# Attention's score loop in phases of three tiles, with part of the fills moved to VectorE

## What is computed

```python
x = L0_attn_x                                    # (8, 1024, 256) float32
x = x + 0.5 * ffn(_layernorm(x), ...)            # 8 experts, top 2, and a shared one
x = x + attn(_layernorm(x), ...)
x = x + 0.5 * ffn(_layernorm(x), ...)

def attn(x, ...):                                # H, DH = 16, 64
    h = layernorm(x) * ln_scale + ln_bias
    c_q, c_kv = h @ w_down_q.T, h @ w_down_kv.T  # 256 -> 128 each
    q, k = rope(heads(c_q @ w_up_q.T)), rope(heads(c_kv @ w_up_k.T))
    v = heads(c_kv @ w_up_v.T)
    attn = softmax(q @ k.T / 8, axis=-1)         # 1024 x 1024 for each head
    return (attn @ v).reshape(b, s, H * DH) @ w_out.T + x
```

## Time and profile before

| | us |
|---|---|
| time, median of 3 runs | 4272.12 (4264.85 to 4278.15) |
| the profiled execution's own time | 4275.68 |
| its span in the trace | 4273.9 |
| attention, first to last fill | 584.5 to 3708.0 |
| one period of attention | 6.11 |

### The profile page before, as it was taken

One profiled execution on the slowest core, in us unless ns is written; L12 is line 12 of the kernel. 1 busy time (PEld: TensorE's weight loads), 2 busy tenths in 40 slices (PEclk: granted clock), 3 DMA queues, 4 the chain that ended last, 5 costly groups with the idle time before them and its releaser, 6 DMA issues. The chain is left out here.

```text
span 4273.9 us, 65982 instructions
## 1 busy us (share of the span) xinstructions
PE 3974.6 (93%) x24896; PEld 2240.6 (52%) x24896; DVE 2681.9 (63%) x3451; ACT 3002.4 (70%) x3792; POOL 3043.7 (71%) x1642
## 2 busy tenths in 40 slices
PE   7999979999999999999998999999999999779999
PEld 6888834444444444444444444444444444368888
DVE  5556567666656666766666666667766666255663
ACT  4444458777877787787778787878787778634454
POOL 3444458778888887887788888878888888624444
PEclk9999989999999999999999999999999999889999
DMA  3333221112111211121112112111211222123331
GB/s 105 107 119 110 72 89 58 53 53 80 53 51 55 76 53 54 60 70 51 59 60 65 63 51 70 58 53 57 79 50 51 66 68 63 31 94 119 119 110 60
DMA packets 194222, 301.07 MB, mean 70 GB/s; under 512 B 51470, under 2 KB 102256, under 8 KB 193264
## 3 DMA queue, kind: packets, MB, share of 16 engines
q1 hardware_dynamic: 193904, 296.86, 21.5%
HBM read 201.86 MB, written 26.74 MB: 53 GB/s over the span
## 5 line engine op out<-in xcount | busy, mean ns | idle before, releaser
L1032 DVE TENSOR_REDUCE atNM<-atPS 128x2 f32<-128x1024 f32 x1024 | 1208.0, 1219 | 788.3 <-PE atPS L848 784.6
L1115 POOL TENSOR_TENSOR atACC<-atACC,atPT 128x1024 f32<-128x1024 f32 x512 | 1290.7, 2521 | 64.3 <-ACT atPT L970 10.3
L970 ACT ACTIVATE atPT<-atPS 128x1024 f32<-128x1024 f32 x1024 | 992.6, 1022 | 201.5 <-PE atPS L869 196.4
L961 ACT ACTIVATE atPS<-atSH 128x1024 f32<-128x1024 f32 x1024 | 1008.7, 1022 | 29.3 <-DMA atSH<-atMD 21.8
L880 PE MATMUL atPO<-atPT,atV 128*64 128x512 f32 x4096 | 980.2, 600 | 0.0
L1115 POOL TENSOR_TENSOR atACC<-atPT 128x1024 f32<-128x1024 f32 x256 | 617.7, 2413 | 145.2 <-PE atOT L891 124.5
L848 PE MATMUL atPS<-atKH,atQH 64*128 64x512 f32 x2048 | 462.3, 449 | 163.6 <-ACT atPT L970 137.3
L1094 POOL TENSOR_TENSOR atVT<-atVT,atSIN 128x512 f32<-128x512 f32 x254 | 347.0, 1366 | 301.1 <-DMA atVT<-atR 300.8
L880 PEld LDWEIGHTS atPO<-atPT,atV 128*64 128x64 f32 x4096 | 283.1, 138 | 482.2 <-issue 475.6
L869 PE MATMUL atPS<-atQH,atKL 64*128 64x512 f32 x2048 | 468.7, 454 | 25.9 <-ACT atPS L961 25.9
L848 PEld LDWEIGHTS atPS<-atKH,atQH 64*128 64x128 f32 x2048 | 194.4, 186 | 413.5 <-ACT atPT L970 349.3
(11 more groups left out here) (275 smaller groups left out, 6552.3 us busy)
## 6 DMA issues: line engine op xcount, KB each, us to landing
atSH<-atMD SPq DMA_DIRECT2D x128, 512.0 KB, 4.4
atVT<-atR SPq DMA_DIRECT2D x508, 128.0 KB, 2.0
f1GB<-f1GD SPq DMA_DIRECT2D x128, 256.0 KB, 6.9
atRSUM<-atRD SPq DMA_DIRECT2D x128, 256.0 KB, 3.9
f2GB<-f2GD SPq DMA_DIRECT2D x128, 256.0 KB, 6.9
X<-x SPq DMA_DIRECT2D x4, 1024.0 KB, 6.0
XS<-x SPq DMA_DIRECT2D x16, 256.0 KB, 3.5
atRQ<-atRSUM SPq DMA_DIRECT2D x256, 4.0 KB, 1.8
```

The lines of the kernel that those rows point to most:

```text
L961: act.eng.activation(PS[ring.of[("score", n, t, j)]][:, :, :], SH[t][:, :, :], ACT.Copy).then_inc(filled[j % 2].sem)
L970: act.eng.activation(PT[k % NPT][:, :, :], PS[ring.of[step]][:, :, :], ACT.Exp, scale=SCALE).then_inc(grown.sem)
L1032: dve.eng.tensor_reduce(NM[:, q // 4, :, q % 4, t], PS[ring.of[step]][:, :, :], AX.X, ALU.max, negate=True).then_inc(most_out.sem)
L1115: pool.eng.tensor_tensor(total[:, :, :], begun[:, :, :], PT[k % NPT][:, :, :], ALU.add).then_inc(gathered.sem)
```

## The change

The list is built from phases of three tiles. With x as the running number of a tile (16 for each head), one turn of the new loop stands for three tiles: score x, maximum, score x + 1; then the others of tick x, the fill of x + 2 and the attend of x - 1; then maximum, score x + 2, maximum; then the others of tick x + 1, the fills of x + 3 and x + 4, the attends of x and x + 1, and the others of tick x + 2. Each old period is two ticks: `begin` and `early` go to the even one, `late` and `end` to the odd one. The maxima run 14 tiles ahead of the scores. `high` of the keys moves from tick 0 to the tick in front, `high` of the queries from the end of the period to tick 0. Key tiles 3 and 7 are filled by VectorE, with a semaphore of their own. `norm` works on one tile at a time at eight periods, not on two at four. `NAT` is 4. The core of the diff:

```diff
-    NAT = 3
+    NAT = 4
...
-                        for i in range(4):
-                            at(end, m, -33 + i, ("norm", b, i))
+                        for k in range(T):
+                            at(end, m, -33 + k, ("norm", b, k))
...
-                at(early, m, 0, ("high", m, 1))
-                at(end, m, 0, ("high", m, 0), ("klow", m))
+                at(end, m, -1, ("high", m, 1))
+                at(early, m, 0, ("high", m, 0))
+                at(end, m, 0, ("klow", m))
...
+            def tile(name, x):
+                n, r = divmod(x, 2 * T)
+                return [(name, n, r // T, r % T)] if 0 <= n < NN else []
+
+            def most_of(x):
+                n, r = divmod(x + 14, 2 * T)
+                return [("most", n, r // 2, r % 2)] if 0 <= n < NN else []
...
-            for g in range(-PER * 2 - 2, PER * NN + 3 * PER):
...
-                order += begin.get(g, []) + scores + mosts + early.get(g, []) + fills + attends
-                order += [("gather",) + s[1:] for s in attends if s[3] % 4] + late.get(g, []) + end.get(g, [])
+            for x in range(-42, 2 * PER * (NN + 4), 3):
+                order += tile("score", x) + most_of(x) + tile("score", x + 1)
+                order += others_of(x) + tile("fill", x + 2) + tile("attend", x - 1)
+                order += [step for step in tile("gather", x - 1) if step[3] % 4]
+                order += most_of(x + 1) + tile("score", x + 2) + most_of(x + 2)
+                order += others_of(x + 1) + tile("fill", x + 3) + tile("fill", x + 4) + tile("attend", x) + tile("attend", x + 1)
+                order += [step for i in range(2) for step in tile("gather", x + i) if step[3] % 4] + others_of(x + 2)
...
+            def filler(j):
+                return 2 if j % 4 == 3 else j % 2
...
+                    elif name == "fill" and filler(step[3]) == 2:
+                        _, n, t, j = step
+                        before = ring.before[("score", n, t, j)]
+                        dve.wait_ge(*shift[t](n))
+                        dve.wait_ge(*(grown if before[0] == "score" else most_out)(*before[1:]))
+                        dve.eng.tensor_copy(PS[ring.of[("score", n, t, j)]][:, :, :], SH[t][:, :, :]).then_inc(filled[2].sem)
```

More of the change, by code:

```diff
@@ L630, in attention @@
             PER = 8
-            begin, early, late, end = {}, {}, {}, {}
+            begin, early, late, end = ((0, 0), {}), ((0, 1), {}), ((1, 0), {}), ((1, 1), {})
             def at(table, m, period, *steps):
-                table.setdefault(PER * (m - 1) + period, []).extend(steps)
+                (tick, _), steps_of = table
+                steps_of.setdefault(2 * (PER * (m - 1) + period) + tick, []).extend(steps)
             TURNS = [(-21, late), (-20, late), (-17, early), (-17, late), (-9, early), (-9, late), (-8, early), (-8, late)]
@@ L680, in attention @@
                 at(end, NN - 4, 3 + i, ("stats", NB, i))
-                at(end, NN - 4, 10 + i, ("norm", NB, i))
+            for k in range(T):
+                at(end, NN - 4, 10 + k, ("norm", NB, k))
             at(end, NN - 4, 7, ("spread", NB))
-            order = []
-            for g in range(-PER * 2 - 2, PER * NN + 3 * PER):
-                n, r = divmod(g, PER)
-                t, pair = r // 4, (2 * (r % 4), 2 * (r % 4) + 1)
-                scores = [("score", n, t, j) for j in pair] if 0 <= n < NN else []
-                n1, r1 = divmod(g - 1, PER)
-                attends = [("attend", n1, r1 // 4, 2 * (r1 % 4) + i) for i in range(2)] if 0 <= n1 < NN else []
-                m, q = divmod(g - 1, PER)
-                mosts = [("most", m + 1, q, i) for i in range(2)] if 0 <= m + 1 < NN else []
-                n2, r2 = divmod(g + 1, PER)
-                fills = [("fill", n2, r2 // 4, 2 * (r2 % 4) + i) for i in range(2)] if 0 <= n2 < NN else []
-                order += begin.get(g, []) + scores + mosts + early.get(g, []) + fills + attends
-                order += [("gather",) + s[1:] for s in attends if s[3] % 4] + late.get(g, []) + end.get(g, [])
+            def tile(name, x):
+                n, r = divmod(x, 2 * T)
+                return [(name, n, r // T, r % T)] if 0 <= n < NN else []
@@ new lines, in most_of, with others_of @@
+            def most_of(x):
+                n, r = divmod(x + 14, 2 * T)
+                return [("most", n, r // 2, r % 2)] if 0 <= n < NN else []
+            def others_of(x):
+                return [step for (tick, _), table in (begin, early, late, end) if tick == x % 2 for step in table.pop(x, [])]
+            order = []
+            for x in range(-42, 2 * PER * (NN + 4), 3):
[5 more added lines that the diff above has]
+                order += [step for i in range(2) for step in tile("gather", x + i) if step[3] % 4] + others_of(x + 2)
@@ L698, in events @@
+            assert not any(table for _, table in (begin, early, late, end))
             def events(*names):
                 return [step[1:] for step in order if step[0] in names]
+            def filler(j):
+                return 2 if j % 4 == 3 else j % 2
             SEQ = {(0, 0): 0, (1, 0): 1, (1, 1): 2, (0, 1): 3}
@@ L734, in attention @@
             shift = [sig(f"shift{t}", 16).expect(heads) for t in range(2)]
-            filled = [sig(f"filled{i}").expect([s for s in events("fill") if s[2] % 2 == i]) for i in range(2)]
+            filled = [sig(f"filled{i}").expect([s for s in events("fill") if filler(s[2]) == i]) for i in range(3)]
             score, grown = (sig(x).expect(events("score")) for x in ("score", "grown"))
@@ L916, in scalar @@
                         act.wait_ge(*turned(b - 1, 1, 1))
-                        for k in (2 * i, 2 * i + 1):
-                            one, two = (slice(x * T + k, x * T + k + 1) for x in range(2))
-                            ins = act.eng.activation(Y[:, k, :], X[:, k, :], ACT.Identity, scale=A[:, two], bias=B[:, two])
-                            if b < NB:
-                                ins = act.eng.activation(X[:, k, :], X[:, k, :], ACT.Identity, scale=A[:, one], bias=B[:, one])
-                        if i == 3:
+                        one, two = (slice(x * T + k, x * T + k + 1) for x in range(2))
+                        ins = act.eng.activation(Y[:, k, :], X[:, k, :], ACT.Identity, scale=A[:, two], bias=B[:, two])
+                        if b < NB:
+                            ins = act.eng.activation(X[:, k, :], X[:, k, :], ACT.Identity, scale=A[:, one], bias=B[:, one])
+                        if k == T - 1:
                             ins.then_inc(normed.sem)
@@ L955, in scalar @@
                         act.eng.activation(ML[t][:, :], OT[0:8, 0:128], ACT.Copy).then_inc(row_out.sem)
-                    elif name == "fill":
+                    elif name == "fill" and filler(step[3]) < 2:
                         _, n, t, j = step
@@ L1147, in sync @@
                         sp.wait_ge(*written(n, t))
-                        for i in range(2):
-                            sp.wait_ge(*filled[i].past(n - 1, t, T - 2 + i))
+                        for j in range(T - 3, T):
+                            sp.wait_ge(*filled[filler(j)].past(n - 1, t, j))
                         sp.eng.dma_start(SH[t][:, :, :].rearrange("p h q -> p (h q)"),
```

6 lines of the change are left out of this document (3 added, 3 removed).

## The result

| | us |
|---|---|
| changed kernel, median of 4 runs | 4487.9 (4485.7 to 4498.3) |
| kernel before, on the same chip | 4269.1 (4264.9 to 4278.2) |
| ratio, 95% interval | 1.0514 (1.0489 to 1.0539) |
| profiled execution, changed | 4498.3, span 4496.5 |
| predicted | 4430 (4240 to 4560) |

The kernel is 5.1% slower. The sign and the place were forecast; the loss is 219 us, not 160.

What follows compares the result with a forecast made beforehand. TensorE plus one wait per period was taken as the bound. Per triple, -0.78 - 0.12 + 0.90 + 0.42 + 0.05 = +0.47 us, x 341 = +160 us, gave 4430 us, range 4240 to 4560.

Steps and rivals of the forecast that it cites:

- The sign and the place: Slower, chance 0.75; in attention, the fill of the middle score of the second phase (B) comes late.
- the clock: Rival: TensorE idles more and part of attention runs at 1.2 GHz; a tenth would cost some 290 us; chance 0.03.
- -0.78: TensorE's work for three tiles in attention falls from 6.56 to 5.78 us, the mid-phase wait for exponentials gone.
- gap A: After phase A (score, maximum, score), with one attend: B's middle score waits for its fill, 0.90 us per triple.
- gap B: After phase B (maximum, score, maximum), with two attends: late fills and accumulator copies cost 0.42 us per triple.
- -0.12 for earlier roundings: At head starts, TensorE's waits for the rounded queries go away, 0.12 us per triple.
- the 9.64 of the forecast: Predicted time of one triple (three tiles) in attention, 9.64 us, against 9.17 before.
- tick 8: Triples starting at this tick: a rotation stands before VectorE's fill and makes it late, 1.5 us.
- The neighbourhood of attends 7 and 0: At ticks 7 and 15 the second attend waits for ScalarE's copy of the accumulator, 1.3 and 1.9 us.
- the forecast's 0.47: Net loss per triple in attention, +0.47 us, times 341 triples +160 us.
- VectorE's fill: VectorE's 128x1024 copy from SBUF to PSUM, not in the trace, taken at 1.21 us like the reduction.
- my rival on the faster side: Phases cover the fill of B's middle score, waits under 0.85 us a triple; 153 us faster, 4120 us; chance 0.17.

Runs made afterwards that it cites:

- VectorE's fills first: Changed kernel with only VectorE's fills moved in front of the other steps of their tick, ScalarE's still behind them: 4415.8 us, ratio 1.0336.
- three moves: Changed kernel with the broadcast right behind the write, the accumulator's copy before ScalarE's fills, VectorE's fills before the other steps: 4349.6 us, ratio 1.0188.

## Why the prediction was right, and where it was not

**Right: the mechanism and the place.** The wait for exponentials fell to 4.1 us, and in its place scores wait for fills and attends for the copy. The size, 4488 against 4430, owes part to luck: the waits were taken too large, which nearly cancels a gain taken too large, and the clock was left out.

**What goes away: too large.** The wait itself was 137.3 - 4.1 = 133 us, 0.39 us a triple. The forecast's -0.78 also took TensorE's own work in the new order at 5.78 us. The first score and maximum of a triple hold to it: 1.03 us forecast, 1.07 on average. But in the plain place above, the work of gap A takes 2.13 us (2743.39 to 2745.52), not 1.96, since the switch to an attend and back takes 0.17 us that I left out. In gap B at ticks 1 and 5, where nothing waits, the forecast's terms give 2.79 + 0.93 + 0.20 = 3.92 us (values, a row) and 2.79 + 0.91 + 0.91 = 4.61 (a projection, half an output projection); measured are 4.07 and 4.68. So the gain was taken too large by about 0.3 us a triple.

**The roundings: not shown.** The -0.12 for earlier roundings did take away a wait of before, 14.5 us in all:

```profile
PE atPS L848 <- ACT atQH L950: 14.5, 25, 0.6
```

But in the old order the same edit, together with the fourth buffer that was priced at nothing, cost 32 us. No run shows the 41 us that 0.12 a triple would be.

**The waits: too large as well.** Forecast were 0.90 in gap A and 0.42 in gap B, 1.32 us a triple; measured are 1.05. Gap A has 0.63, not 0.90. Where ScalarE fills, the plain place has 0.76 us (2745.52 to 2746.28), not 1.05, and projections 0.32 to 0.55, not 0.63; behind rotations and roundings it is 2.28 for 2.7 at tick 9, 1.05 for 1.2 at tick 0 and 1.37 for 2.0 at tick 15. The whole gap A came out near the forecast all the same: expected 1.96 us of TensorE's work, a third of the 2.6 us of others (0.87) and 0.95 for waits and restarts, 3.78; measured 3.69. The wait taken too long made up for the switch left out. That this wait moves with its cover is shown by two runs (0.63 to 0.16, 0.47 to 0.12). Neither of them was faster.

**Gap B: the waits right in sum, not one by one.** Expected: 0.69 + 0.23 + 1.87, two thirds of the others (1.74) and 0.42 of waits, 4.95 (with 1.03 and 3.78 in front, and 0.12 off for the earlier roundings, the 9.64 of the forecast); measured 5.07, with 7.34 at tick 15. Of it 0.24 are waits for fills and 53 us or 0.16 a triple waits for the copy, 0.40 against 0.42. One term was put at nothing wrongly: "the transfers behind a row keep their two ticks ahead of the first fill that they feed". They keep their ticks, but a tick lies elsewhere now: in triples that start at 12 and 13, and at 4 for the second half, the fill of key tile 0 stands soon behind them. ScalarE waited 99.3 us for the transfer (70 us in front of fills of the first half, 29 in front of those of the second), not 21.8, and 29 us came back when it was issued earlier. Other terms of gap B were smaller than forecast, such as tick 8, with 0.52 instead of 1.5. The neighbourhood of attends 7 and 0, which was foreseen, is worth some 20 us.

**The clock: a rival that was partly true.** I gave it 0.03 and priced it at nothing in the sum. After the long wait at tick 9 TensorE's matmuls run slower for a while (order in time; then two stretches of it, in the columns of the earlier trace rows, where the number behind the five engines is the granted clock):

```profile
2380.72 0.50 PE L888 MATMUL atPS<-atQH,atKL 64*128 64x512 f32 x2 [2.40 <-DVE atPS L1056]
2381.06 0.39 PE L888 MATMUL atPS<-atQL,atKH 64*128 64x512 f32 x2
...
2383.12 0.79 PE L888 MATMUL atPS<-atQH,atKL 64*128 64x512 f32 x2 [1.21 <-ACT atPS L979]
2383.71 0.63 PE L888 MATMUL atPS<-atQL,atKH 64*128 64x512 f32 x2
```

```profile
2381.60:2382.30 0.70, 0.31 (x4) 0.00 (x0) 0.34 (x1) 0.26 (x1) 0.70 (x2) 1.00 0.39 67
...
2383.00:2384.50 1.50, 1.38 (x6) 0.83 (x6) 1.50 (x2) 1.01 (x2) 1.49 (x1) 0.50 0.02 7
```

The same pair of matmuls takes 0.39 us and, after two waits of 2.40 and 1.21 us, 0.63. The granted clock is 1.00 before and 0.50 after, the lower level, 1.2 GHz. It shows in the averages too: at tick 9 gap B takes 5.08 us though no fill is late in it; with VectorE's fills first, where the wait at tick 9 is 0.45 and not 2.28, the same gap takes 4.08. Not every such wait is followed by it, as I took for granted ahead of the run with VectorE's fills first: the changed kernel has 38 stretches at 0.50 in attention, 13 of them begin in the 22 triples of tick 9 and 13 in those of tick 15. In these stretches TensorE is busy 169 us, before it was 38 us (11 stretches). A matmul takes 0.32 us in these stretches on average and 0.16 elsewhere, so I estimate the price of the clock at (169 - 38) / 2 = 65 us, 0.19 us a triple. TensorE's busy time grew by 43 us, since its other work shrank a little.

Per triple, the forecast's 0.47 changes by -0.27 (waits), about +0.3 (own work) and 0.19 (clock), to about 0.7; measured are 0.66. In the run with three moves the clock is back at 0.99 and TensorE's busy time at 2937 us, with nothing done about the clock itself:

```profile
580.00:3782.00 3202.00, 2936.88 (x18615) 1342.98 (x18611) 2304.87 (x2456) 2252.25 (x2723) 2555.57 (x1284) 0.99 0.18 58
```

**VectorE's fill.** Taken at 1.21 us, it took 1.22 (1204/1218/1230 ns); it does not spread as the rotations do, which agrees with the Trainium skill's rule on one SBUF input (SBUF — State Buffer, section Who interferes with whom). The Trainium skill's advice to rotate matmul groups through PSUM banks (Perfetto Trace Analysis, section Optimizing Tensor Performance), my rival on the faster side, is kept by the phases. The reading of one buffer did overlap the next group's matmuls, and 133 us of waits for exponentials went. But here a fill must follow it in the same buffer before the group after that, and the waits for fills grew by 281 us.

**Open.** Even with three moves a triple takes 9.39 us against 9.17 of the old order. The difference is idle time: 265 us in attention against 185, with TensorE's busy time 10 us less than before (2937 and 2947). The table above splits it: fills 192, shared bank 36, copy 33. That the waits move between these shares when a fill is moved is shown. That three buffers force it, whatever the order, is not.

## What to carry to other kernels

Before a wait is traded away, count, for every buffer that is handed on, the whole chain until its next user (read, reduce, refill) against the work that stands between, in the new order and tick by tick, and do it for transfers and for single shared banks too. Try a placement in both orders before a loss is put down to one of them: what cost 119 us in one order gained 72 in the other. When a loop's step is changed from two tiles to three, everything whose distance was counted in periods gets three distances instead of one, and the shortest one has to be priced.

## What was not expected of the hardware

Pairs of matmuls went from 0.39 to 0.63 us, at a granted clock of 0.50, after idle times of 2.40 and 1.21 us with 1.2 us of work between. So waits of this length can cost more than themselves: by the estimate above 65 us in attention, at a mean clock of 0.97.
